# The FFN of a decoder layer on one core: features 4 to 6 of block 0 ahead of the down-weight jobs, and the x2 loads of blocks 1 and 2 issued earlier

## The reference, cut to what matters

```
x = layernorm(x + attention(x, Wq, Wk, Wv, Wo, Wdown, Wup))      # 16 heads of 32, low-rank projections
x = layernorm(x + recurrence(x, ctx, ctx, decay))               # r = d*r + k*v, out = q*r along the sequence
gate_w, up_w = spline(gate_cp), spline(up_cp)                    # (2048, 512) each
down_w = spline(down_cp)                                         # (512, 2048)
x = layernorm(x + (silu(x @ gate_w.T) * (x @ up_w.T)) @ down_w.T)
```

## Time and profile before

| | |
|---|---|
| times of 3 runs | 626.8, 627.12, 628.09 us, median 627.12 |
| the profiled execution's own time | 628.18 us |
| its span, first to last instruction | 626.3 us |
| busy: PE, DVE, ACT, POOL | 96%, 66%, 57%, 46% of the span |
| mean granted TensorE clock | 0.995 of full speed |
| chain that ended last | PE 85%, DVE 5%, ACT 3%, DMA 3% |

### The profile page before, as it was taken

One profiled execution on the slowest core, in us unless ns is written; L12 is line 12 of the kernel. 1 busy time (PEld: TensorE's weight loads), 2 busy tenths in 40 slices (PEclk: granted clock), 3 DMA queues, 4 the chain that ended last, 5 costly groups with the idle time before them and its releaser, 6 DMA issues.

```text
span 626.3 us, 12076 instructions
## 1 busy us (share of the span) xinstructions
PE 601.2 (96%) x4292; PEld 474.3 (76%) x4292; DVE 412.8 (66%) x842; ACT 359.5 (57%) x1026; POOL 286.5 (46%) x344
## 2 busy tenths in 40 slices
PE   8999999999999999999998798899899999999995
PEld 8778887888887978888877586676677677767663
DVE  3365676777677767776767955666586658556644
ACT  5665756666665767666757845544455645544351
POOL 0728189889775777849557551164002100200111
PEclk9999999999999999999999998999999999999999
DMA  9622002615241042102133287544806741684011
GB/s 320 230 69 101 2 2 102 177 53 177 85 136 68 3 146 78 48 32 79 46 116 92 102 212 178 174 102 93 227 17 155 217 100 28 158 218 69 2 67 68
DMA packets 34571, 68.09 MB, mean 109 GB/s; under 512 B 14160, under 2 KB 16336, under 8 KB 33744
## 3 DMA queue, kind: packets, MB, share of 16 engines
q1 hardware_dynamic: 29296, 52.51, 29.4%
q0 software_dynamic: 4928, 14.29, 7.4%
q10 hardware_dynamic: 288, 0.52, 0.3%
HBM read 42.14 MB, written 13.93 MB: 90 GB/s over the span
## 4 chain that ended last, share of the span: by engine, by line
PE 85%; DVE 5%; ACT 3%; DMA 3%; SPq 1%; issue 1%; POOL 0%; POOLq 0%; ACTq 0%; DVEq 0%
PE bank L464 16%; PE bank L466 14%; PE bank L465 14%; PE bank L651 8%; PE bank L1509 7%; PE bank L639 5%; PE bank L673 5%; PE bank L1484 4%; PE bank L1418 2%; DMA x_in<-x 2%; SPq L1449 1%; ACT probs L840 1%; PE bank L659 1%; PE bank L690 1%; PE bank L563 1%
## 5 line engine op out<-in xcount | busy, mean ns | idle before, releaser
L840 ACT ACTIVATE probs<-bank,minus_max 128x256 f32<-128x256 f32 x256 | 118.6, 487 | 38.9 <-DVE minus_max L1007 38.6
L1007 DVE TENSOR_REDUCE minus_max<-bank 128x2 f32<-128x512 f32 x128 | 79.5, 682 | 46.3 <-PE bank L639 46.3
L1018 DVE COPY probsT<-bank 128x512 f32<-128x512 f32 x96 | 59.8, 677 | 19.7 <-PE bank L651 19.6
L1698 DVE TENSOR_TENSOR hidden<-bank,silu 128x512 f32<-128x512 f32 x64 | 44.0, 687 | 42.5 <-PE bank L466 26.0
L651 PE MATMUL bank<-ident,probs 128*128 128x128 f32 x512 | 62.5, 273 | 3.1 <-ACT probs L840 3.1
L651 PEld LDWEIGHTS bank<-ident,probs 128*128 128x128 f32 x512 | 57.0, 140 | 7.4 <-ACT probs L840 5.0
L1653 ACT CAST hidden_hi_lo<-hidden 128x512 fp32r<-128x512 f32 x64 | 39.8, 621 | 38.6 <-DVE hidden L1698 38.2
L1647 ACT ACTIVATE silu<-bank 128x512 f32<-128x512 f32 x64 | 38.1, 596 | 38.0 <-PE bank L466 37.3
L1702 DVE TENSOR_TENSOR hidden_hi_lo<-hidden,hidden_hi_lo 128x512 fp32r<-128x512 f32 x64 | 44.4, 694 | 23.4 <-ACT hidden_hi_lo L1653 22.6
L1782 POOL TENSOR_TENSOR ffn_var_eps<-ffn_mean_var,constants 128x4 f32<-128x4 f32 x3 | 0.6, 200 | 125.6 <-DVE ffn_mean_var L1732 125.6
L1509 PE MATMUL bank<-hidden_hi_lo,down_raw 64*128 64x512 f32 x384 | 55.8, 409 | 0.7 <-DVE outs_T L1711 0.6
(11 more groups left out here) (201 smaller groups left out, 1594.4 us busy)
## 6 DMA issues: line engine op xcount, KB each, us to landing
features_by_group<-features_by_cell SPq DMA_DIRECT2D x128, 128.0 KB, 2.3
ctx_squared_T<-in_ctxT SPq DMA_DIRECT2D x8, 512.0 KB, 5.8
xres<-in_x SPq DMA_DIRECT2D x8, 512.0 KB, 4.5
x_in<-x SPq DMA_DIRECT2D x16, 256.0 KB, 3.3
makers_out<-makers_rounded SPq DMA_DIRECT2D x9, 416.0 KB, 4.8
xin_T<-in_xT SPq DMA_DIRECT2D x7, 512.0 KB, 4.0
x<-x_rows SPq DMA_DIRECT2D x7, 512.0 KB, 5.0
x_residual<-x POOLq DMA_DIRECT2D x3, 1024.0 KB, 6.9
```

The costliest lines, as they stand in the source:

```text
L840: inc(nc.scalar.activation(probs[:, g, t, :], S[g][:, t * T:(t + 1) * T], ACT.Exp, bias=nmax[:, g, t:t + 1], accum_out=rsum[:, t, g:g + 1] ...
L1007: inc(nc.vector.tensor_reduce(nmax[:, g, :], S[g][:].rearrange("p (t k) -> p t k", t=TT), AX.X, ALU.max, negate=True), "max")
L1018: inc(nc.vector.tensor_copy(probsT[:, g, :, :], S[g][:].rearrange("p (k t) -> p k t", k=2)), "ptv")
L1698: inc(nc.vector.tensor_tensor(hm[:], U[:], sg[:], ALU.mult), "hm")
```

## The change

Three things are moved; no arithmetic is added or left out.

1. Block 0's features 4, 5 and 6 go ahead of jobs 21 and 22 in half (0,1): on PE ahead of the jobs' matmuls, on ACT ahead of the cast of `hidden` and of both job copies, on DVE likewise. Feature 7 stays behind the jobs on PE; its cast and subtraction go between the two parts of the jobs.
2. Block 1's x2 tiles get four buffers: tiles 2 and 3 go into `yq`. Their loads wait for nothing and are issued with those of tiles 0 and 1, tile 2 ahead of maker 11 and tile 3 ahead of maker 12. `s_x2in` has four semaphores.
3. Block 2's tiles 0 and 1 are loaded between the first and the second quad of block 1's feature copies; before, they came after the second quad and after the store of the last batch.

```diff
     def pe_xt(pe, n, t, out):
-        pe.wait_ge(s_x2in[t % 2], 16 * (2 * n + t // 2 + 1))
+        pe.wait_ge(s_x2in[t], 16 * n + 16)
...
+    def x2in_of(n, t):
+        return yq[:, t, :] if n == 1 and t >= 2 else x2in[:, t % 2, :]
+
     def sp_x2in(sp, n, t):
-        if t >= 2 or n:
+        if t < 2 and n == 2:
+            sp.wait_ge(s["xt"], BT + t + 1)
+        elif t < 2 and n:
+            wait(sp, "xt", BT * (n - 1) + t + 3)
+        elif t >= 2 and n != 1:
             wait(sp, "xt", BT * n + t - 1)
         if t == 0:
             sp.wait_ge(s["x2st"], 32 * n + 32)
-        sp.dma_start(x2in[:, t % 2, :], x2_d[:, BT * n + t, :]).then_inc(s_x2in[t % 2], 16)
+        sp.dma_start(x2in_of(n, t), x2_d[:, BT * n + t, :]).then_inc(s_x2in[t], 16)
...
             pe_turn(pe, n, st, j, 0)
+            if n == st == 0 and j == 1:
+                for i in (4, 5, 6):
+                    pe_features(pe, 0, i, OWN[i])
             pe_fill(pe, n, st, j)
...
             if n == st == 0 and j == 1:
-                for i, out in OWN.items():
-                    pe_features(pe, 0, i, out)
+                pe_features(pe, 0, 7, OWN[7])
...
+            if n == st == 0 and j == 1:
+                for i in (4, 5, 6):
+                    act_fh(act, 0, i, OWN[i])
             act_hh(act, n, st, j)
             for i in jobs:
                 act_job(act, i, job_bank(i))
+            if n == st == 0 and j == 1:
+                act_fh(act, 0, 7, OWN[7])
...
+            if n == st == 0 and j == 1:
+                for i in (4, 5, 6):
+                    dve_fl(dve, 0, i, OWN[i])
             dve_hl(dve, n, st, j)
             for i in jobs:
                 dve_job(dve, i, job_bank(i))
+            if n == st == 0 and j == 1:
+                dve_fl(dve, 0, 7, OWN[7])
             for i in jobs:
                 dve_job_lo(dve, i)
             dve_turn(dve, n, st, j, 1)
-            if n == st == 0 and j == 1:
-                for i, out in OWN.items():
-                    dve_fl(dve, 0, i, out)
...
             sp_makers_out(sp, 10)
-            for t in range(2):
+            for t in range(3):
                 sp_x2in(sp, 1, t)
             sp_makers_out(sp, 11)
+            sp_x2in(sp, 1, 3)
             sp_makers_out(sp, 12)
             sp_store(sp, B - 2)
```

More of the change, by code:

```diff
@@ L451, in program @@
     s_msg = [sem(f"s_masks_hidden{i}") for i in range(2)]
-    s_x2in = [sem(f"s_x2_in{i}") for i in range(2)]
+    s_x2in = [sem(f"s_x2_in{i}") for i in range(BT)]
     s_feat = [sem(f"s_features{g}") for g in range(NG)]
@@ L1387, in pe_xt @@
         for k in range(KT):
-            last = nc.tensor.transpose(out[:, k * P:(k + 1) * P], x2in[:, t % 2, k * P:(k + 1) * P], ident[:])
+            last = nc.tensor.transpose(out[:, k * P:(k + 1) * P], x2in_of(n, t)[:, k * P:(k + 1) * P], ident[:])
         inc(last, "xt")
@@ L1688, in act_step @@
             act_turn(act, n, st, j, 1)
-            if n == st == 0 and j == 1:
-                for i, out in OWN.items():
-                    act_fh(act, 0, i, out)
     def dve_hm(dve, n, st, j):
@@ L2011, in _ @@
             for n in range(1, NB):
-                for t in range(2, BT):
-                    sp_x2in(sp, n, t)
+                if n > 1:
+                    for t in range(2, BT):
+                        sp_x2in(sp, n, t)
                 for half_ in range(2):
@@ L2017, in _ @@
                             sp_features(sp, n, g, c)
-                if 1 < n < NB - 1:
+                if n < NB - 1:
                     for t in range(2):
@@ L2025, in _ @@
                     sp_store(sp, B - 1)
-                    for t in range(2):
-                        sp_x2in(sp, n + 1, t)
             for g in range(QUAD, NG):
```

## The result

The kernel before took 628.10 us in the median of 20 runs (the lowest 626.17, and one stray of 3284), the changed kernel 626.37 us (20 runs, 625.41 to 630.82). The ratio is 0.9976 with an interval of 0.9966 to 0.9987: 1.5 us off, between 0.8 and 2.1. The forecast named the right events and gave nearly each the wrong size.

The account below looks back on a forecast made before the run. PE, busy 96%, was taken to bound the kernel, with SP's copy queue setting 377.94 to 387.85. Terms 0.6 + 1.5 + 1.8 - 1.5 gave 2.4 us off 627.12, so 624.7 us, range 622.9 to 626.4.

Parts of the forecast that it names:

- -1.5 us: Group 4 of block 0: PE's clock at 0.50 after one gathered wait of 3.8 us, costing 1.5 us.
- two such stretches: Group 4: upper bound of the clock loss, 3.4 us, if PE's clock stays at 0.50 for two stretches.
- 0.6 us, not 3: Block 0: SP's second quad starts at 377.3 instead of 377.94, held by job 22's predicated copy; gain 0.6 us.
- 1.46 us. I take 1.5 us: Block 1, third transpose: the 1.68 us wait for tile 2 goes, DVE is late next; gain 1.5 us, between 0 and 1.7.
- 397.1: Block 1: landing time of maker 11 with 256 KB put ahead of it, so job 27 does not wait.
- the loads only change places: Rival, block 1: part 2 gives nothing, 626.2 us; same if part 1 gives nothing and low clock costs 2.4; chance 0.15.
- 1.77 us: Block 2, first transpose: the wait for its load goes with the early loads; gain 1.77 us, at least 1.4.
- not after 1.68 and 1.77: Kernel before: the clock fell after the 2.17 us wait but not after the two waits for x2 loads.
- 0.55, 0.17 and 0.08: Chances of the forecast itself, of no clock fall, and of the feature part failing (625.3 us), summed into "faster".
- No clock fall: Rival, group 4: the clock does not fall or recovers during the wait; gain 3.9, 623.2 us; chance 0.17.
- slower through the clock: Rival, group 4: the clock stays at 0.50 from 387.2 to 397.5 or more; 628.4 us and up; chance 0.05.
- cost the end nothing: Kernel before, 378.23 to 381.65: the low clock lost 1.71 us, but in front of a wait for SP.

Follow-up runs that it names:

- e3: The full change plus 18 filler matmuls keeping PE busy in the wait ahead of group 4, against the kernel before; 624.41 us, ratio 0.9937.
- e2: Part 1 alone (features 4 to 6 moved, loads as before), against the kernel before; 628.25 us, ratio 1.0012.
- e12: The full change once more, for a second trace, against the kernel before; 626.67 us, ratio 0.9973.
- e4: The full change with block 0's second quad copied group by group instead of cell by cell, against the kernel before; 627.95 us, ratio 0.9991.
- e10: Part 1 alone plus the 18 filler matmuls ahead of group 4, against the kernel before; 628.11 us, ratio 0.9998.
- e5: The full change with SP's block 0 queue (copies, tiles, makers) rewritten in the order PE needs them, against the kernel before; 621.24 us, ratio 0.9888.
- e1: Parts 2 and 3 alone, features 4 to 7 behind the jobs as before, against the kernel before; 624.84 us, ratio 0.994.
- e9: Part 3 alone (block 2's tiles 0 and 1 loaded early), against the kernel before; 625.13 us, ratio 0.9944.
- e7: e1 with maker 11 issued ahead of tiles 2 and 3 of block 1, against the kernel before; 624.63 us, ratio 0.9939.
- e13: Part 2 alone (four buffers and earlier loads for block 1), against the kernel before; 627.00 us, ratio 0.9991.
- e15: A further trace of the kernel before, nothing edited; the traced execution took 628.95 us.
- e16: A further trace of the kernel before, nothing edited; the traced execution took 628.08 us.
- e8: The kernel before, unedited, traced again and measured against itself; 627.25 us, ratio 0.9990.
- e14: A further trace of the kernel before, nothing edited; the traced execution took 626.51 us.
- e6: e5's order of SP's queue, but features 4 to 7 behind the jobs, against the kernel before; 623.75 us, ratio 0.9923.
- e11: e5 with POOL's 512 KB segment table load issued four gate and up products later, against the kernel before; 620.15 us, ratio 0.9865.

## Why the prediction was right and wrong

The events came as forecast; the step that failed is the size of all four terms of the sum. Part 2 was put at 1.5 us and is worth 0 to 0.6; part 3 at 1.8 and is worth 3.0; part 1 at 0.6 and is worth 0.3; the clock at -1.5 and costs 2.0 to 2.7. Behind three of the four stands one error: a wait, or a clock that did or did not fall, was read in one execution and taken for the kernel's.

- **Right: what moves and where.** SP's second quad starts at 377.15 (I wrote 377.3); DVE's predicated copies of job 22 end just ahead of it, at 377.05, so `ws` binds and not feature 4. The stall before feature 7 is gone, PE is at group 4 at 382.75 (383.4) and goes on at 387.06 (387.2), after 4.31 us (3.8). Both load waits are gone, job 27 has none, and 2.7 us of clock loss stand behind group 4.

- **Wrong in size: "-1.5 us" for the clock.** It measured -2.7 by the trace and -2.0 by e3. I priced the wait by the one fall in the trace, 3.42 us after a wait of 2.17. My upper bound, "two such stretches", is the length that came, less the part that lay on the wait. The length of the wait does not decide it alone: e2's wait of 4.24 us was followed by one stretch of 3.41, e12's of 4.25 by 6.83. The loss depends on the execution, and the bound deserved more weight than "near the one row there is". The wait of 2.17 us that I set beside the rule of the Trainium skill was one for DVE, not for a DMA, and in ten traces that have it the clock fell after it in eight.

- **Wrong in size: part 1, "0.6 us, not 3".** The start of attention differs by up to half a microsecond between executions, so I count from SP's first feature copies of block 0. Before:

```profile
358.70 1.21 SPq L1449 DMA_DIRECT2D features_by_group<-features_by_cell  x2
```

  and after:

```profile
358.17 1.21 SPq L1449 DMA_DIRECT2D features_by_group<-features_by_cell  x2
```

  The second quad starts 19.24 us behind this before and 18.98 after: 0.3 us of gain. The other nine traces with the old place have 19.25 to 19.27; of the eight with the new one six have 18.75 to 19.04, and e4 and e10 have 19.42 and 19.49. The term missed that ACT's cast of feature 4 now has to wait for a landing, of the last copies of the first quad:

```profile
373.25 1.56 ACT L1433 CAST features_by_cell<-bank 128x512 fp32r<-128x512 f32 x3 [0.34 <-DMA features_by_group<-features_by_cell]
```

  DVE's three subtractions start 0.18 us idle behind it, and the copies of job 22 behind those:

```profile
373.87 1.89 DVE L1438 TENSOR_TENSOR features_by_cell<-bank,features_by_cell 128x512 fp32r<-128x512 f32 x3 [0.18 <-ACT features_by_cell L1433]
375.67 0.68 DVE L1713 TENSOR_TENSOR hidden_hi_lo<-hidden,hidden_hi_lo 128x512 fp32r<-128x512 f32 x1
376.27 0.78 DVE L1332 COPY_PREDICATED weights_now<-features_by_group,bank 128x256 f32<-128x256 uint8 x2
```

  That wait is 0.30 to 0.39 us in five of the eight, 0.79 and 0.84 in e4 and e10, and absent in e5. I had followed the queues of the engines, and not the reader of the memory that the moved casts write. Part 1 alone makes nothing faster (e2), and 0.3 us of gain with 2 or more of clock loss is why the full change is 1.5 us slower than its own parts 2 and 3 (e1); with the clock kept (e3, 624.41) it is level with them (624.84).

- **Wrong in size: part 2, "1.46 us. I take 1.5 us".** The row of 1.68 us is the largest of six: 0.38 (e9), 0.44, 0.57, 0.72 and 0.88 are the others with the old order and the old feature place. It goes with the landing of the load: 8.00 us in the first trace, 6.70 to 7.22 in those five. I took one execution's wait as the kernel's. What goes returns in part for DVE (0.53 to 0.56 in e7, e13 and the changed kernel) or for maker 11 (1.22 in e1). For maker 11 my "397.1" was 395.0 in the full change and 398.6 in e1. The 0.9 us for the 256 KB put ahead of it don't show as such: with the tile ahead it took 7.2 and 6.9 us from its issue in e13 and e3, and 7.0 to 7.9 in the traces with the old order, so all that it lost is the 0.5 us or so that SP takes to issue the tile. e13 gives 0.6, and e1 is 0.3 below e9: between 0 and 0.6. Of my rivals "the loads only change places" was nearest, and most of all its second form, that part 1 gives nothing and the low clock costs 2.4.

- **Wrong in size: part 3, "1.77 us".** It measured 3.0 alone (e9; 3.5 by the ratio). That the clock fell "not after 1.68 and 1.77" was true of one trace. Of eight traces that have this wait the clock fell after it in three (e13, e15, e16) and not in five (the first, e2, e8, e10, e14). If the 41 runs of 75 are those in which it fell, the load's lateness costs 1.8 + 1.5 x 41/75 = 2.6 us on average, and 3.3 against the median, which is a run with the fall. The count is an estimate: e7 and e9 have a mean clock of 0.993 in their traces with no fall at 450.

- **The sum.** 0.3 + 0.3 + 3.0 - 2.3 (the middle values) is 1.3 us, against 1.5 measured. My terms were too high by 0.3 and 1.2, too low by 1.2, and the loss too low by 0.8. That the errors of parts 2 and 3 cancel is luck; part 1 and the clock are what is missing. The range was luck as well: its upper end lets part 2 alone fail, while my own lower bounds for all terms together (0, 0, 1.4 and -3.4) would have made the kernel 2 us slower. And 0.55, 0.17 and 0.08 less a tenth are 0.72, not the 0.77 that I wrote for "faster".

- **The rivals.** "No clock fall" is excluded by both traces of the full change; "slower through the clock" too: the clock is back at 392.42. The forecast that the low clock of before "cost the end nothing" holds for the fall at 378: e8 and e14 have no fall there, wait 2.07 and 2.06 us for group 4 and not 0.5, and reach it at 387.57 and 387.42, as before.

What stays open: why one program's transfers land at different times (tile 2 after 6.7 to 8.0 us, the first quad's last copy after 3.8 to 4.6, maker 11 of e1 after 8.7); why the fall at 450 comes in some executions only; and whether part 1 can gain more than 0.3 us in the old order of SP's queue, since e10 moved the features with the clock kept and gained nothing.

## What to carry to other kernels

Small waits that are gathered into one in front of work can cost more than they did apart: ask for the clock after the wait, and let the range hold more than one stretch like the one that was seen (here it was one in e2 and two in the changed kernel and e12). When a queue of transfers bounds the stretch, work moved ahead of it only lengthens a wait; order that queue by the time of need first (4.8 us off in e6, 3.8 by the early loads alone in e1), and only then move the work (2.5 us more in e5; in the queue's old order the move took 1.5 off the gain of e1). A wait for a transfer that is read in one execution has a spread: look at it in three or four before a term of 1.5 us is made of it.

## What the runs showed of the hardware

- Waits of nearly one size do or don't lower the clock. After 2.2 us at feature 7 it fell in the first look, e15 and e16, and not in e8 and e14 (in eight of all ten traces with that wait); after 1.8 to 2.1 us at 450 in two of five looks at the kernel before. One unchanged program thus has two groups of times 1.6 us apart.
- After 4.2 to 5.4 us it stayed at 0.50 for 6.8 us in e4, e12 and the changed kernel, but for 3.4 in e2, after 4.24 us.
- A load of one queue delays that of another. With nothing but POOL's 512 KB table moved away (e11 against e5), SP's 416 KB load of maker 11 took 5.5 us to land and not 6.8. With the second quad copied cell after cell it took 5.7, 5.8 and 6.1 us where the table went 1.1 to 1.5 us behind it (the changed kernel, e12, e2), and 6.9 to 8.7 in the eleven other traces, where the table went between 0.2 us ahead and 0.3 behind the earlier trace rows. The Trainium skill (DMA: Bandwidth & Descriptors, "Queues, rings and completion order") says that each DMA engine takes turns between the queues that it has work for; these rows agree.
